# A decoder's two small attentions on one core: VectorE takes a head's row maxima ahead of the pieces of other batches

## What is computed

```python
# L0 cross-attention
q = (x @ Wq).reshape(b, n, N_HEADS, HEAD_DIM)
k, v = jnp.split(ctx @ Wkv, 2, axis=-1)
...
logits = jnp.einsum('bqhd,bkhd->bhqk', q, k) * scale
w = jax.nn.softmax(logits, axis=-1)
attn = jnp.einsum('bhqk,bkhd->bqhd', w, v)
...
return attn @ Wout + bout
# L1 self-attention
scores = jnp.einsum('bqgsd,bkgd->bgsqk', q, k) * scale
scores = jnp.where(causal, -jnp.inf, scores)
attn = jax.nn.softmax(scores, axis=-1)
ctx = jnp.einsum('bgsqk,bkgd->bqgsd', attn, v)
return ctx @ Wo + bo
```

## Time and profile before

| | |
|---|---|
| median of 3 runs | 3309.2 us |
| lowest, highest | 3295.82, 3311.93 us |
| the profiled execution | 3292.8 us |
| its span, first to last instruction | 3291.0 us |
| its mean granted PE clock | 0.96 |
| PE, DVE, ACT, POOL busy | 86%, 64%, 54%, 43% |

### The profile page before, as it was taken

The page is one execution under the profiler, slowest core; times in us unless marked ns, Lnnn a source line. Parts: engine busy times, 40 slices in busy tenths (PEclk is TensorE's granted clock), DMA queues, the critical chain, the costliest instruction groups (busy, mean ns, idle before and its releaser), DMA issues. The chain is left out here.

```text
span 3291.0 us, 64401 instructions
## 1 busy us (share of the span) xinstructions
PE 2830.0 (86%) x24866; PEld 2007.4 (61%) x24866; DVE 2091.4 (64%) x4481; ACT 1764.0 (54%) x3844; POOL 1419.4 (43%) x1539
## 2 busy tenths in 40 slices
PE   3999999965888886999999968888999999975786
PEld 1666666643666665777777756666666766652343
DVE  4676776656788775655555547765555565555896
ACT  3555555544887885332233257764444444454785
POOL 0444444423888884544445425451111122212563
PEclk9999999997899997999999989999999999997999
DMA  4000000010000012100000011002000110022000
GB/s 167 1 1 1 1 1 1 1 42 27 2 2 2 2 47 73 46 8 7 1 1 1 1 49 40 21 2 71 14 33 33 39 40 1 1 71 77 14 20 26
DMA packets 45077, 81.49 MB, mean 25 GB/s; under 512 B 5603, under 2 KB 15845, under 8 KB 44646
## 3 DMA queue, kind: packets, MB, share of 16 engines
q1 hardware_dynamic: 44774, 77.38, 6.9%
HBM read 73.18 MB, written 4.19 MB: 24 GB/s over the span
## 5 line engine op out<-in xcount | busy, mean ns | idle before, releaser
L1099 POOL TENSOR_TENSOR c_pT<-c_prob,c_pT 128x512 f16<-128x512 f32 x256 | 296.1, 1172 | 92.4 <-ACT c_pT L1051 90.2
L1974 POOL TENSOR_TENSOR c_prob<-c_prob,c_inv 128x512 f32<-128x512 f32 x128 | 133.4, 1043 | 310.7 <-DVE c_inv L2198 310.7
L754 DVE SCALAR_TENSOR_TENSOR a_pT<-psT,a_kvh_t,a_pT 128x256 f16<-128x256 f32 (+1 forms) x256 | 94.6, 411 | 169.7 <-ACT a_pT L663 169.7
L1099 POOL TENSOR_TENSOR a_pT<-a_prob,a_pT 128x384 f16<-128x384 f32 x128 | 120.8, 950 | 160.0 <-ACT a_pT L1051 159.4
L1371 DVE TENSOR_REDUCE c_peak<-psS 128x2 f32<-128x512 f32 x256 | 171.0, 685 | 29.6 <-PE psS L1202 26.6
L1290 ACT ACTIVATE c_prob<-psT 128x512 f32<-128x512 f32 x256 | 155.2, 607 | 55.7 <-PE psT L1221 35.8
L465 POOL TENSOR_TENSOR a_q_rot<-a_q_cos,a_q_sin 128x512 f32<-128x512 f32 x64 | 81.0, 1266 | 194.6 <-DVE a_q_sin L773 194.6
L1051 ACT CAST c_pT<-c_prob 128x512 f16<-128x512 f32 x256 | 159.1, 622 | 0.0
L2122 ACT CAST c_pT<-psT 128x512 f16<-128x512 f32 x128 | 74.9, 585 | 140.4 <-PE psT L1986 140.4
L484 POOL TENSOR_TENSOR a_prob<-a_prob,a_inv 128x128 f32<-128x128 f32 x128 | 52.3, 409 | 214.3 <-DVE a_inv L747 214.3
L2114 ACT ACTIVATE c_prob<-psS,c_negmax 128x256 f32<-128x256 f32 x256 | 119.4, 475 | 44.3 <-DVE c_negmax L2191 40.5
(11 more groups left out here) (632 smaller groups left out, 11373.7 us busy)
## 6 DMA issues: line engine op xcount, KB each, us to landing
c_feed<-in_L_ffn_w1T SPq DMA_DIRECT2D x16, 512.0 KB, 3.6
c_feed<-in_L_ffn_w2T SPq DMA_DIRECT2D x16, 512.0 KB, 3.5
x_all<-in_x SPq DMA_DIRECT2D x1, 4096.0 KB, 14.3
a_stage<-in_L_attn_WqT SPq DMA_DIRECT2D x8, 512.0 KB, 7.4
a_stage<-in_L_attn_WoutT SPq DMA_DIRECT2D x8, 512.0 KB, 10.0
a_feed<-in_L_xattn_Wq SPq DMA_DIRECT2D x8, 512.0 KB, 3.7
c_feed<-in_L_xattn_Wo SPq DMA_DIRECT2D x8, 512.0 KB, 4.0
c_feed<-in_L_ffn_w3T SPq DMA_DIRECT2D x8, 512.0 KB, 3.6
```

The lines of the kernel that those rows point to most:

```text
L754: last = dve.scalar_tensor_tensor(pT[1][:, r, m, m * P:N], T[:, m * N + m * P:(m + 1) * N], kvh_t[:, b % 2, m, H + h:H + h + 1], pT[0][:, ...
L1099: pool.tensor_tensor(pT[1][:, c % NPH, :], prob[:, c % NPX, :], pT[0][:, c % NPH, :], ALU.subtract)\
L1974: pool.tensor_tensor(prob[:, h % NPB, :, :], prob[:, h % NPB, :, :], inv[:, h % NPB, :].rearrange("p (n a) -> p n a", a=1).broadcast_to([P ...
```

## The change

On DVE the block with `rowmax` and `fill_slots` moves from behind the pieces of step t - 1 to the front of step t. Nothing else in the program is different.

```diff
                 for t in range(FIRST, LAST):
+                    if (found := peak_head(t)) is not None:
+                        b, h = found
+                        rowmax(b, h)
+                        if h % GH == GH - 1:
+                            fill_slots(b, h // GH)
                     for kind, b, n in pieces_at(t - 1):
                         if kind in ("x", "o", "v", "kv") or (kind == "q" and not from_ctx):
                             low(b, kind, n)
@@
                             move_stack(dve.tensor_copy, b, n).then_inc(s.bank_dve, 1)
                         elif kind == "y":
                             measure(b, n)
-                    if (found := peak_head(t)) is not None:
-                        b, h = found
-                        rowmax(b, h)
-                        if h % GH == GH - 1:
-                            fill_slots(b, h // GH)
                     if (found := pv_head(t - 1)) is not None and found[1] % GH == GH - 1:
                         rows_of(found[0], found[1] // GH)
```

## The result

The changed kernel has the median 3294.5 us (3290.0 to 3302.1, 19 runs), the kernel before 3302.7 (3292.1 to 3311.9, 19 runs) on the same chips. The ratio is 0.9978, with the 95% interval 0.9970 to 0.9986: some 7 us gained. I had forecast 3324 and a range from 3296 to 3346.

The account below looks back on a forecast made before the run. No engine alone was taken as the bound; PE waits for whichever engine lags. attn1's 13.6 us plus xattn0's 1 made about 15 us later, carried from the 3309.2 median to 3324 us, range 3296 to 3346.

Parts of the forecast that it names:

- the ring: xattn0: each copy waits behind a maximum, whose scores wait for the copy before; PE delays of 1.2, 0.4 and 1.3 us.
- the stall: xattn0, six of seven batches: FILL blocked 4.22 us by POOL, PE idle 3.14 us before the peaks' transposes; expected to go.
- The waits for the maxima (L1202): Sign in both stages: PE's waits for row maxima, 13.6 us in xattn0 and 5.8 in attn1, nearly gone.
- The waits for L1281 at L1160 and L1177: Sign in xattn0: PE's waits for copied stacks rise 2 to 3 us a batch; under 1.5 means the forecast is wrong.
- Net for a batch 0.4 - 0.3 = 0.1 us: xattn0: 0.4 us lost at x pieces and q0, 0.3 gained at the peaks' transposes; 1 us later over seven batches.
- PE's clock falls in the long stall: xattn0: argument for the faster case, that several short waits may be cheaper than one long; given no separate size.
- Rival 1: xattn0: delayed copies cost PE under 1.5 us, not 3, so most of 20.6 us is won; 3296 us, chance 0.17.
- Rival 2: xattn0: FILL stays blocked through the POOL run, 20 us on top; 3344 us, chance 0.17.
- rival 3: Whole kernel: projections hide the delayed pieces and the maxima gained are off the path; no change, 3309 us, chance 0.11.
- Forecast 13.6 us later: attn1 in sum: 7.5 + 1 + 6.3 - 1.2 = 13.6 us later.
- The x pieces: attn1, batch start: x pieces come later, delaying kv0; 1.5 us in five batches, 0.5 in two, 7.5 + 1 us.
- The stack: attn1: the sk1 copy falls behind a maximum, the next stack's transpose goes 0.9 us later; 6.3 us over seven batches.

Follow-up runs that it names:

- b_again: The kernel before, unchanged, run and profiled a second time: 3302.9 us, ratio 1.0004 to before, span 3299.3 us.
- no_fill_new: Against the kernel before: in xattn0 maxima go first and are written negated straight into q_stack, without FILL; attn1 unchanged. 3281.5 us, ratio 0.9931.
- warm_before: Kernel before, old order, plus 28 unused PE matmuls in each of xattn0's batches 2 to 7 before the peaks' transposes: 3291.0 us, ratio 0.9967.

## Why the prediction was wrong, and where it was right

**The baseline.** The sum was made on a profiled execution of 3292.8 us and carried over to a median of 3309. I noted the 16 us between them and took them for scatter. Some 9 of them were in one place, xattn0's batches, 61.4 us in place of 59 to 60, and there they are PE's clock: 0.89 in a batch of b_again, 0.97 and 0.92 in turns in the short execution. The change removes this, and a sum on the short execution could not see this half. Of the 18.1 us that xattn0 gains, 8.9 are there against the short execution too (452.5 to 443.6), and those it could have seen.

**xattn0, the ring: right in the mechanism.** Expected were waits handed out to the copies in steps 10 to 12 and a net of next to nothing at the peaks' transposes. Measured: 0.1 us later (13.9 against 13.7 from the end of q1), where I had 0.3 earlier; waits of 0.88, 1.35 and 0.70, FILL 0.23 us. Counted from q1, the three transposes that wait for a copy start 1.2, 2.3 and 3.4 us later than before; I had 1.2, 1.6 and 2.9. That the ring costs as much as the stall was worth up to that point holds, and no_fill_new shows it without the stall: 21.4 us. Two of my signs did not come as I wrote them. The waits for the maxima (L1202) were to be nearly gone and are 8.3 and 2.3 us. The waits for L1281 at L1160 and L1177 were to rise by 2 to 3 us a batch, under 1.5 being a sign of error; they rose by 9.4 us in seven batches, 1.3 each. Another 8.5 us, on which none of my signs counted, stand before the rotated parts at L1160.

**xattn0, the end of the sum: this is the step that failed.** I closed the account at the peaks' transposes, with "Net for a batch 0.4 - 0.3 = 0.1 us". Behind them lies PE's own work, and PE's clock was low there: 2.3 us a batch by the rows above, and with the later low stretch 3.3. I had named it, "PE's clock falls in the long stall", and put it under rival 1 without a price, though the profile that I summed on had eight transposes at 1.03 us right behind the stall and 0.61 where PE had not waited, and 7.7 or 6.5 us from there to the end of y0 in place of 5.2. The term for the clock behind the stall was put at nothing: +1 us stood for -18, or for -9 on the execution that I used. warm_before shows that in the old order, with the stall as long as ever, the clock alone is worth 14 us. Rival 1 asked for copies that cost less than I counted, with the transposes of o in step 12 under 1.5 us later; they are 3.4 later. Its time, 3296, was nearly right, by luck, for a reason that it had only as an aside.

**Rival 2 (FILL stays blocked) and rival 3 (nothing moves): out.** FILL is short in step 12 in every batch where it was 4.2 us, and both stages moved, by -18.1 and +10.6 us.

**attn1: right in sign and place, slightly large.** Forecast 13.6 us later, measured 10.6. The x pieces: forecast 8.5, with 1.5 a batch since I took FILL to be blocked; it is not (0.20 us), and kv0 is 1.0 late, the lower of my bounds. Undoing the new order there gives back 3.6 us. The stack: forecast 6.3, 0.9 a batch; the wait for it is 3.1 us in all, 0.5 at most, and undoing the new order there gives 4.2 together with kv1's piece. So 7.8 of the 10.6 stand at the two groups of steps that were undone, and 2.8 in none.

**Sum.** -18.1 + 10.6 = -7.5 us, where +1 + 13.6 = +14.6 was forecast. The lower end of my range, 3296, is 1.5 us above the measured median.

## What to carry to other kernels

Before costing a reordering, hold the profiled execution against the spread of the runs: if it lies at an edge, a second profile shows which stage is not always the same, and that stage has a price of its own. When a stall goes, go on with the sum behind it until PE is back at its full clock, since the work after a long wait is part of the wait's price. And where an instruction of 16 elements takes 4 us, change its form before changing its place: moving it got 18 us net in its stage, since the order alone costs 21 there, and another form of it, left in its place, got 42.

## What was not expected of the hardware

FILL waited through four POOL instructions, 4.2 us, and not only for the one in flight, in six batches of every kernel that keeps it in its old place in xattn0 as a product (five profiles); the Trainium skill, "SBUF — State Buffer", section "SBUF: two separate sides", has the one that comes second wait for the whole instruction of the first. In other steps the same FILL came in behind the first of them (0.73 to 0.75 us in before), although POOL's next instruction followed without a gap. What decides between the two was not found. And 168 matmuls whose results nobody reads made the kernel 11 us faster, by keeping PE's clock up through a wait that they did not shorten.
